# Second layer: the attention's values two slots ago, moved ahead of the scores on TensorE and their read ahead of the exponents on ScalarE

## The chip, the cores and the metric

The kernel runs on one core of one Trainium2 chip. The metric is the device time of the whole kernel in microseconds (us), as the median of several runs. Everything is computed in 32-bit floats apart from a few small helpers.

Engine names in the profile: PE is TensorE (matmuls; PEld are its weight loads), DVE is VectorE, ACT is ScalarE, POOL is GpSimd, SP is SyncE.

## The reference

Two transformer decoder layers over 16 sequences of 256 tokens of width 256 (4096 tokens). The change lies in the self-attention of the second layer:

```python
x = x + _L0_attn_ref(_layernorm(x, axis=-1), ...)
x = x + _L0_xattn_ref(_layernorm(x, axis=-1), ctx_1024, ...)
x = x + _L0_ffn_ref(_layernorm(x, axis=-1), ...)
x = x + _L1_attn_ref(_layernorm(x, axis=-1), L1_attn_Wq, L1_attn_Wkv_down, L1_attn_Wk_up, L1_attn_Wv_up, L1_attn_Wo)
x = x + _L1_xattn_ref(_layernorm(x, axis=-1), ctx_1024, ctx_1024, ...)
x = x + _L1_ffn_ref(_layernorm(x, axis=-1), L1_ffn_w_gate, L1_ffn_w_up, L1_ffn_w_down)

def _L1_attn_ref(x, Wq, Wkv_down, Wk_up, Wv_up, Wo):      # 8 heads of 64, latent width 64
    q = (x @ Wq.T).reshape(b, t, N_HEADS, HEAD_DIM)
    kv_latent = x @ Wkv_down.T
    k = (kv_latent @ Wk_up.T).reshape(b, t, N_HEADS, HEAD_DIM)
    v = (kv_latent @ Wv_up.T).reshape(b, t, N_HEADS, HEAD_DIM)
    scores = jnp.einsum('bqhd,bkhd->bhqk', q, k) * HEAD_DIM ** (-0.5)
    attn = jax.nn.softmax(scores, axis=-1)
    out = jnp.einsum('bhqk,bkhd->bqhd', attn, v)
    return out.reshape(b, t, N_HEADS * HEAD_DIM) @ Wo.T
```

## The kernel before

The program has four parts one after another: the first layer's attentions, its experts, `layer1` (the second layer's two attentions), and `feed_forward`. Only `layer1` is touched.

`layer1` works through eight groups g of 512 tokens (two sequences each). A group has eight slots s, one for each sequence b and pair of heads m; the slots are counted through all groups as t = 8g + s, and the last is t = 63 (`TAIL`). The keys' and values' up-projections are folded into the weights, so each slot multiplies absorbed queries with the 64-wide latent rows.

The order on each engine is written out by hand, as one loop over t for each engine, and each engine runs its row in order. Semaphores tie the rows together. What one slot's attention needs, in order:

- `scores(t)` (L1854, PE) fills banks P[0] and P[1]. It waits until the exponents of slot t-1 have read them.
- `maxima(t, e)` (L2206, DVE), one for each of the two heads e.
- `exponents(t)` (L2089, ACT), four of them, into `pr[t % 2]`, with their sums.
- `invert(t)` (L2211, DVE), and the product with the inverse sums (L1795, POOL), four of them.
- `turn(t)` (L1865, PE) transposes the rows into P[2] and P[3]. In the PE loop it stands in slot t+1.
- `by_key(t)`, the two copies of the turned rows into `PT[t % 2]`: ACT copies P[2] (L2102), DVE copies P[3] (L2217). Both stand in slot t+1 too, ACT's behind everything that ACT keeps in that slot.
- `values(t)` (L1880, PE) multiplies them with the latent rows into P[4]. It waits for both copies (`PTa_ready`, `PTd_ready`) and for the read of the slot before (`aT_ready`). In the PE loop it stands in slot t+2.
- `heads(t)` (L2096, ACT) reads P[4], also in slot t+2.

The other work of the layer is spread over the slots of a group as extras: in slot 0 the turn of the cross attention (L1966), the queries' fourth part (L1939) and the cross attention's values (L1977); in slot 1 the turn of the next group's normalised rows (L1890); in slot 2 the projection of the second sequence of the group before (L1948); in slot 3 the next group's latent (L1925); in slot 4 a turn of normalised rows, one of the latent keys (L1932) and queries; in slot 5 queries and a turn; in slot 6 queries and the cross attention's scores (L1958); in slot 7 a projection. They write the three banks P[5] to P[7] in turn; ACT empties most of them (`keep_unit`, L2077), and an extra waits until its bank is empty. ACT also normalises rows (L2115) at the end of slots 3 and 4.

Of the kernel before, what the change touches and what calls it, by code (L numbers as in the profile page):

```python
# [1581 lines left out]
def layer1(nc, ctx, c, io, dr):  # L1582

    st = ExitStack()
    with st:
# [67 lines left out]
        def group_step(t):  # L1653
            return t // NS, t % NS

        def there(i):
            return 0 <= i < NG
# [11 lines left out]
        TAIL = NS * Z + NS - 1  # L1669
# [59 lines left out]
        def wait_kept(e, name, i, parts=None):  # L1729
            k, _, n = place[name, i]  # L1730
            e.wait_ge(kept[k], n + (parts or after[name]))
# [3 lines left out]
        with nc.Block(no_gpsimd_drain=True) as block:  # L1735
# [79 lines left out]
            def _(p):  # L1815
# [25 lines left out]
                def scores(t):  # L1841
                    g, s = group_step(t)
                    b, m = s // NP, s % NP
                    if t == 0:
                        p.wait_ge(q.l_kept, 3 * (NG - NEARLY))
                        p.wait_ge(q.l_out_kept, NG - NEARLY)
                    if b == 0:
                        wait_kept(p, f"q{m}", g)
                    for u in range(2):
                        for e in range(2):  # L1850
                            if t and u == 0:
                                p.wait_ge(q.exp_ready, 4 * (t - 1) + 2 * e + 2)
                            r = slice(LR * e, LR * e + LR)
                            x = p.matmul(P[e][:, S * u:S * u + S], qT[g % 2][r, m, S * b + 128 * u:S * b + 128 * u + 128],  # L1854
                                         latT[g % 2][r, S * b:S * b + S], start=True, stop=True, tile_position=(LR * e, 0))
                    x.then_inc(q.s_psum, 1)
# [12 lines left out]
                def values(t):  # L1869
                    g, s = group_step(t)  # L1870
                    b = s // NP
                    if s == 0:
                        wait_kept(p, "latk", g)
                    p.wait_ge(q.PTa_ready, t + 1)
                    p.wait_ge(q.PTd_ready, t + 1)
                    if t:
                        p.wait_ge(q.aT_ready, t)
                    for k in range(2):
                        for e in range(2):
                            x = p.matmul(P[4][LR * e:LR * e + LR, 0:S], lat[g % 2][:, 2 * b + k, :], PT[t % 2][:, e, k, :],  # L1880
                                         start=(k == 0), stop=(k == 1), tile_position=(0, LR * e), skip_group_check=True)
                    x.then_inc(q.a_psum, 1)
# [59 lines left out]
                def project(i, b):  # L1942
                    name = f"project{b}"
                    p.wait_ge(q.aT_ready, NS * i + NP * b + NP)
                    room(p, name, i)
                    for j in range(2):
                        for m in range(NP):
                            x = p.matmul(bank(name, i)[:, D * j:D * j + D], aT[:, m, S * b + 128 * j:S * b + 128 * j + 128], wb[:, m, :],  # L1948
                                         start=(m == 0), stop=(m == NP - 1))
                    x.then_inc(full(name, i), 1)  # L1950
# [35 lines left out]
                for t in range(TAIL):  # L1986
                    g, s = group_step(t)
                    late, behind, ahead = there(g - 2), there(g - 1), there(g + 1)
                    scores(t)
                    if t == 0:  # L1990
                        queries(0, 1)
                        queries(0, 2)
                    if t >= 1:
                        turn(t - 1)
                    if t >= 2:
                        values(t - 2)
                    if s == 0 and late:
                        x_turn(g - 2)
                    if t == 1:
                        queries(0, 3)  # L2000
                    if s == 0 and behind:
                        queries(g, 3)
                    if s == 1 and ahead:
                        turn_norm(0, g + 1)
                    if s == 2 and behind:
                        project(g - 1, 1)
                    if s == 3 and ahead:
                        latent(g + 1)
                    if s == 4 and late:
                        turn_norm(2, g - 2)  # L2010
                    if s == 4 and ahead:
                        latent_keys(g + 1)
                    if s == 5 and ahead:
                        queries(g + 1, 1)
                    if s == 6 and ahead:
                        queries(g + 1, 2)
                    if s == 0 and late:
                        x_values(g - 2, 0)
                        x_values(g - 2, 1)
                    if s == 4 and ahead:  # L2020
                        queries(g + 1, 0)
                    if s == 5 and behind:
                        turn_norm(1, g - 1)
                    if s == 6 and behind:
                        x_scores(g - 1)
                    if s == 7:
                        project(g, 0)
                scores(TAIL)
                turn(TAIL - 1)
                values(TAIL - 2)  # L2030
                project(Z, 0)
                turn(TAIL)
                x_turn(Z - 1)
# [21 lines left out]
            def _(a):  # L2055
# [27 lines left out]
                def exponents(t):  # L2083
                    for e in range(2):
                        a.wait_ge(q.nmax_ready, 2 * t + e + 1)
                        if t >= 2:
                            a.wait_ge(q.pt_psum, 2 * (t - 2) + e + 1)
                        for u in range(2):
                            a.activation(pr[t % 2][:, e, u, :], P[e][:, S * u:S * u + S], ACT.Exp, bias=nmax[t % 2][:, e, u:u + 1],  # L2089
                                         accum_out=sums[t % 2][:, e, u:u + 1]).then_inc(q.exp_ready, 1)  # L2090

                def heads(t):
                    _, s = group_step(t)
                    b, m = s // NP, s % NP
                    a.wait_ge(q.a_psum, t + 1)
                    a.activation(aT[:, m, S * b:S * b + S], P[4][:, 0:S], ACT.Copy).then_inc(q.aT_ready, 1)  # L2096
# [28 lines left out]
                for t in range(TAIL):  # L2125
                    g, s = group_step(t)
                    late, behind, ahead = there(g - 2), there(g - 1), there(g + 1)
                    exponents(t)
                    if t in (0, 1):
                        keep_unit(f"q{t + 2}", 0, qT[0][:, t + 2, :], bank(f"q{t + 2}", 0)[:, :])  # L2130
                    if t >= 2:
                        heads(t - 2)
                    if s == 0 and late:
                        keep_unit("xturn", g - 2, xPT[:, :], bank("xturn", g - 2)[0:S2, :])
                    if s == 0 and behind:
                        keep_unit("q3", g, qT[g % 2][:, 3, :], bank("q3", g)[:, :])
                    if s == 1 and ahead:
                        keep_norm(0, g + 1, [hT0[:, u, :] for u in range(2)])
                    if s == 3 and ahead:
                        keep_unit("lat", g + 1, latT[(g + 1) % 2][:, :], bank("lat", g + 1)[:, :])  # L2140
                    if s == 4 and late:
                        keep_norm(2, g - 2, [c.hT_all[:, u, T * (g - 2):T * (g - 2) + T] for u in range(2)])
                    if s == 5 and ahead:
                        keep_unit("q0", g + 1, qT[(g + 1) % 2][:, 0, :], bank("q0", g + 1)[:, :])
                        keep_unit("q1", g + 1, qT[(g + 1) % 2][:, 1, :], bank("q1", g + 1)[:, :])
                    if s == 6 and behind:
                        keep_norm(1, g - 1, [hT[:, u, :] for u in range(2)])
                    if s == 6 and ahead:
                        keep_unit("q2", g + 1, qT[(g + 1) % 2][:, 2, :], bank("q2", g + 1)[:, :])
                    if t >= 1:  # L2150
                        by_key(t - 1)
                    if s == 3 and late:
                        normalise(2, g - 2, x5)
                    if s == 4 and behind:
                        normalise(1, g - 1, x4[(g - 1) % 2])
                    if s == 7 and behind:
                        x_exponents(g - 1)
# [839 lines left out]
```

## Time and profile before

| | |
|---|---|
| time, median of 3 runs | 1672.96 us (1669.79 to 1673.18) |
| profiled execution, own time | 1675.36 us |
| its span | 1673.6 us |
| `layer1`'s slots | from 932.9 us to about 1331 us of the span |
| PE busy, over the span | 1536.0 us (92%) |
| DVE, ACT, POOL busy | 979.0, 842.2, 468.4 us |
| mean granted clock of PE | 0.968 |

The page's slices show one fortieth of the span (41.8 us) in each digit; slices 23 to 32 hold the slots of `layer1`:

```profile
PE   8999999998987899999999899999999989996299
ACT  4446555555555422211212565666656533597980
PEclk9999999999998999999999999999999889998599
```

A digit 9 means busy for 90% or more; the line PEclk gives the granted clock in tenths of full speed. An average over a slice hides waits shorter than a few us, so the slots are read one by one below.

### The profile page before, as it was taken

What the parts mean: (1) busy time and instruction counts of PE and PEld (TensorE: products, weight loads), DVE (VectorE), ACT (ScalarE), POOL (GpSimd) and SP (SyncE); (2) the same over time, 40 slices, a digit from 0 to 9 for tenths busy, and PEclk for the clock granted to TensorE, in tenths of its full rate; (3) what the DMA queues carried; (4) which work ended last, traced back from release to release, by engine and by line L of the source; (5) the groups of instructions that cost most, each with busy time, mean ns of one, the idle gap of its engine ahead of it and who ended that gap; (6) DMA issues with size and microseconds to landing.
All of it is one profiled execution on the core that took longest, in us unless ns stands there. A gap on an engine that the chain in (4) does not pass through costs nothing. (4 is left out here: it accounts for less than half of the span.)

```text
span 1673.6 us, 27432 instructions
## 1 busy us (share of the span) xinstructions
PE 1536.0 (92%) x10279; PEld 1083.3 (65%) x10279; DVE 979.0 (58%) x2296; ACT 842.2 (50%) x1849; POOL 468.4 (28%) x592
## 2 busy tenths in 40 slices
PE   8999999998987899999999899999999989996299
PEld 5676767766755777787777466666666654442288
DVE  3665766767766435222222567766664568777883
ACT  4446555555555422211212565666656533597980
POOL 4223234253234410000002665555542300032100
PEclk9999999999998999999999999999999889998599
DMA  3440111011151154334424211110100000000031
GB/s 115 156 156 18 47 30 44 30 47 44 34 165 39 61 164 137 125 113 126 153 87 136 70 39 52 43 34 27 39 14 14 1 25 1 0 1 15 24 99 65
DMA packets 100929, 108.32 MB, mean 65 GB/s; under 512 B 25410, under 2 KB 89804, under 8 KB 100800
## 3 DMA queue, kind: packets, MB, share of 16 engines
q1 hardware_dynamic: 94656, 90.01, 17.3%
q0 software_dynamic: 6144, 16.57, 3.1%
q8 instruction: 83, 1.36, 0.3%
q14 instruction: 46, 0.38, 0.1%
HBM read 64.77 MB, written 42.01 MB: 64 GB/s over the span
## 5 line engine op out<-in xcount | busy, mean ns | idle before, releaser
L1795 POOL TENSOR_SCALAR c_pr<-c_pr,c_rsum 128x256 f32<-128x256 f32 x256 | 128.2, 518 | 190.2 <-DVE c_rsum L2211 189.8
L2089 ACT ACTIVATE c_pr<-bank,c_nmax 128x256 f32<-128x256 f32 x256 | 118.0, 473 | 119.9 <-DVE c_nmax L2206 119.8
L1526 ACT ACTIVATE b_G<-bank 128x320 f32<-128x320 f32 x128 | 56.0, 437 | 210.8 <-PE bank L1475 210.8
L1475 PE MATMUL bank<-b_XT,shared 128*128 128x320 f32 x512 | 154.6, 437 | 0.0
L2206 DVE TENSOR_REDUCE c_nmax<-bank 128x2 f32<-128x512 f32 x128 | 82.4, 685 | 108.6 <-PE bank L1854 108.5
L1489 PE MATMUL bank<-shared,b_G 128*128 128x256 f32 x640 | 142.2, 379 | 0.0
L1489 PEld LDWEIGHTS bank<-shared,b_G 128*128 128x128 f32 x640 | 120.9, 190 | 17.8
L1072 DVE TENSOR_TENSOR hT_all<-bank,a_causal 128x512 f32<-128x512 f32 x128 | 79.4, 682 | 67.5 <-PE bank L563 67.5
L498 POOL TENSOR_TENSOR a_L<-a_L,a_Lm 128x1232 f32<-128x1232 f32 x32 | 72.0, 2249 | 149.5 <-DVE a_Lm L1087 149.5
L1475 PEld LDWEIGHTS bank<-b_XT,shared 128*128 128x128 f32 x512 | 92.5, 193 | 27.6 <-issue 1.2
L1545 DVE COPY b_Y<-bank 128x256 f32<-128x256 f32 x80 | 33.9, 424 | 120.3 <-PE bank L1489 120.1
L1537 DVE COPY b_XT<-bank 128x256 f32<-128x256 f32 x80 | 34.0, 424 | 100.0 <-PE bank L1462 100.0
L1754 POOL MEMSET c_minus<- 128x4 f32 x1 | 0.1, 102 | 309.1 <-POOLq L54 309.1
L1865 PE MATMUL bank<-ident,c_pr 128*128 128x128 f32 x512 | 73.2, 283 | 12.5 <-POOL c_pr L1795 10.0
L2650 PE MATMUL bank<-wdT,d_raw 128*128 128x256 f32 x384 | 83.1, 379 | 0.9 <-DVE d_raw L2897 0.9
L2593 PE MATMUL bank<-hT_all,wuT 128*128 128x512 f32 x192 | 82.9, 593 | 0.0
L2593 PE MATMUL bank<-hT_all,wgT 128*128 128x512 f32 x192 | 82.6, 592 | 0.0
L2650 PEld LDWEIGHTS bank<-wdT,d_raw 128*128 128x128 f32 x384 | 72.9, 190 | 11.0 <-DVE d_raw L2897 1.1
L1865 PEld LDWEIGHTS bank<-ident,c_pr 128*128 128x128 f32 x512 | 55.5, 142 | 37.7 <-POOL c_pr L1795 25.6
L690 PE MATMUL bank<-ident,a_L 128*77 128x128 f32 x512 | 66.9, 282 | 12.4 <-ACT a_L L943 7.2
L1854 PE MATMUL bank<-c_latT,c_qT 64*128 64x256 f32 x512 | 75.5, 407 | 0.6 <-ACT c_qT L2077 0.4
L513 POOL DMA_INDIRECT t_slots_in<-a_h,a_slot_s x64 | 63.3, 989 | 30.0 <-issue 17.1
(376 smaller groups left out, 3400.2 us busy)
## 6 DMA issues: line engine op xcount, KB each, us to landing
shared<-L_ffn_w SPq DMA_DIRECT2D x32, 512.0 KB, 6.0
t_slots_in<-a_h SPq DMA_DIRECT2D x20, 512.0 KB, 7.5
shared<-t_slots_in SPq DMA_DIRECT2D x15, 640.0 KB, 7.3
t_slots_out<-b_Y SPq DMA_DIRECT2D x15, 640.0 KB, 4.1
hT_all<-x SPq DMA_DIRECT2D x8, 512.0 KB, 4.0
a_xr<-x SPq DMA_DIRECT2D x8, 512.0 KB, 3.9
t_x_a<-a_x SPq DMA_DIRECT2D x8, 512.0 KB, 2.9
shared<-t_x_a SPq DMA_DIRECT2D x8, 512.0 KB, 4.3
```

The source lines that it names most:

```text
L498: p.tensor_tensor(L[n % 2][:, :, :], L[n % 2][:, :, :], bcast(Lm[n % 2][:, :], 2, S2), ALU.subtract).then_inc(q.sub_ready, 1)
L690: x = p.transpose(bank(name, i)[0:S2, 128 * k:128 * k + 128], L[n % 2][:, 4 * rg + k, :], ident)
L1072: v.tensor_tensor(A[:, rg, :, :, :].rearrange("p e k t -> p (e k) t"), P[rg][:, :].rearrange("p (n t) -> p n t", t=128), bcast(causal[:, : ...
L1475: t = p.matmul(P[2 + n % 2][:, 0:HC], w1[e % 3][:, u, 128 * f:128 * f + 128], XT[e % 2][:, u, HC * m:HC * m + HC], start=(u == 0), stop=(u ...
L1489: t = p.matmul(P[4 + n % 3][:, 0:D], G[e % 2][:, f, 128 * j:128 * j + 128], w2[e % 3][:, f, :], start=(f == 0), stop=(f == 3))
L1795: p.tensor_scalar(pr[k][:, e, u, :], pr[k][:, e, u, :], rsum[k][:, e, u:u + 1], 1.0, ALU.mult, ALU.mult).then_inc(q.pr_ready, 1)
L1854: x = p.matmul(P[e][:, S * u:S * u + S], qT[g % 2][r, m, S * b + 128 * u:S * b + 128 * u + 128], latT[g % 2][r, S * b:S * b + S], start=Tr ...
L1865: x = p.transpose(P[2 + e][:, S * k + 128 * u:S * k + 128 * u + 128], pr[t % 2][:, e, u, 128 * k:128 * k + 128], ident)
L2089: a.activation(pr[t % 2][:, e, u, :], P[e][:, S * u:S * u + S], ACT.Exp, bias=nmax[t % 2][:, e, u:u + 1], accum_out=sums[t % 2][:, e, u:u ...
L2206: v.tensor_reduce(nmax[t % 2][:, e, :], P[e][:, :].rearrange("p (u k) -> p u k", u=2), AX.X, ALU.max, negate=True).then_inc(q.nmax_ready, 1)
L2593: t = p.matmul(bank[:, :], wT[:, u, 128 * f:128 * f + 128], hT[:, u, T * g:T * g + T], start=(u == 0), stop=(u == 1))
L2650: t = p.matmul(P[n % 8][:, 0:D], raw[:, f, T * g + 128 * j:T * g + 128 * j + 128], wdT[:, f, :], start=(f == 0), stop=(f == FC - 1))
```

## The change

On PE, `values(t - 2)` moves from behind `turn(t - 1)` to ahead of `scores(t)`, in every slot from the third on, and in the tail. On ACT, `heads(t - 2)` moves from behind the exponents (and, in the first slots, a keep) to ahead of them; ACT's tail stays. DVE, POOL and SP keep their rows. No instruction is added or taken out, and all waits stay with their instructions.

```diff
@@ PE
                 for t in range(TAIL):
                     g, s = group_step(t)
                     late, behind, ahead = there(g - 2), there(g - 1), there(g + 1)
+                    if t >= 2:
+                        values(t - 2)
                     scores(t)
                     if t == 0:
                         queries(0, 1)
                         queries(0, 2)
                     if t >= 1:
                         turn(t - 1)
-                    if t >= 2:
-                        values(t - 2)
                     if s == 0 and late:
                         x_turn(g - 2)
...
+                values(TAIL - 2)
                 scores(TAIL)
                 turn(TAIL - 1)
-                values(TAIL - 2)
                 project(Z, 0)
@@ ACT
                 for t in range(TAIL):
...
+                    if t >= 2:
+                        heads(t - 2)
                     exponents(t)
                     if t in (0, 1):
                         keep_unit(f"q{t + 2}", 0, qT[0][:, t + 2, :], bank(f"q{t + 2}", 0)[:, :])
-                    if t >= 2:
-                        heads(t - 2)
```

PE's row in a steady group, from the turn in slot 1 to the turn in slot 3 (L1865 turn, L1880 values, L1890 turn of normalised rows, L1854 scores, L1948 projection). Before:

```order
L1865 MATMUL bank<-ident,c_pr 128x128 x8
L1880 MATMUL bank<-c_PT,c_lat 64x256 x4
L1890 MATMUL bank<-ident,c_h 128x128 x8
L1854 MATMUL bank<-c_latT,c_qT 128x256 x4
L1865 MATMUL bank<-ident,c_pr 128x128 x8
L1880 MATMUL bank<-c_PT,c_lat 64x256 x4
L1948 MATMUL bank<-c_wb,shared 128x256 x8
L1854 MATMUL bank<-c_latT,c_qT 128x256 x4
L1865 MATMUL bank<-ident,c_pr 128x128 x8
```

And after the change, over the same stretch:

```order
L1865 MATMUL bank<-ident,c_pr 128x128 x8
L1890 MATMUL bank<-ident,c_h 128x128 x8
L1880 MATMUL bank<-c_PT,c_lat 64x256 x4
L1854 MATMUL bank<-c_latT,c_qT 128x256 x4
L1865 MATMUL bank<-ident,c_pr 128x128 x8
L1948 MATMUL bank<-c_wb,shared 128x256 x8
L1880 MATMUL bank<-c_PT,c_lat 64x256 x4
L1854 MATMUL bank<-c_latT,c_qT 128x256 x4
L1865 MATMUL bank<-ident,c_pr 128x128 x8
```

The values that stood behind the turn of their slot now close the slot before it: between the turn of a slot's rows and its values stand the extras of one slot alone, where before there were also a set of scores and another turn.

ACT's row over slots 3 and 4 of a steady group (L2089 exponents, L2096 read of the heads, L2077 keeps, L2102 copy, L2115 normalised rows). Before:

```order
L2089 ACTIVATE c_pr,c_sums<-bank,c_nmax 128x256 x4
L2096 ACTIVATE shared<-bank 128x256
L2077 ACTIVATE c_latT<-bank 128x512
L2102 ACTIVATE c_PT<-bank 128x512
L2115 ACTIVATE c_h<-c_x,c_shift,c_rstd 128x256 x4
L2089 ACTIVATE c_pr,c_sums<-bank,c_nmax 128x256 x4
L2096 ACTIVATE shared<-bank 128x256
L2077 ACTIVATE hT_all<-bank 128x512 x2
L2102 ACTIVATE c_PT<-bank 128x512
```

And after:

```order
L2096 ACTIVATE shared<-bank 128x256
L2089 ACTIVATE c_pr,c_sums<-bank,c_nmax 128x256 x4
L2077 ACTIVATE c_latT<-bank 128x512
L2102 ACTIVATE c_PT<-bank 128x512
L2115 ACTIVATE c_h<-c_x,c_shift,c_rstd 128x256 x4
L2096 ACTIVATE shared<-bank 128x256
L2089 ACTIVATE c_pr,c_sums<-bank,c_nmax 128x256 x4
L2077 ACTIVATE hT_all<-bank 128x512 x2
L2102 ACTIVATE c_PT<-bank 128x512
```

The read of the heads stands ahead of the exponents; the copy L2102 keeps its place at the end of the slot's keeps.

## Rows read from the trace of the kernel before

**Rows 1.** Windows, one steady group: length, busy us (count) of each engine, PEclk, DMA share, GB/s

```profile
1127.18:1178.96 51.78, 49.50 (x301) 32.27 (x302) 35.67 (x90) 33.08 (x108) 27.96 (x43) 1.00 0.11 32
```

**Rows 2.** Timeline, DVE, maxima of slots 0 to 7: start, us, engine, line, [idle before]

```profile
1127.18 1.29 DVE L2206 TENSOR_REDUCE c_nmax<-bank 128x2 f32<-128x512 f32 x2 [1.39 <-PE bank L1854]
...
1134.32 1.29 DVE L2206 TENSOR_REDUCE c_nmax<-bank 128x2 f32<-128x512 f32 x2 [2.49 <-PE bank L1854]
...
1138.45 1.29 DVE L2206 TENSOR_REDUCE c_nmax<-bank 128x2 f32<-128x512 f32 x2 [0.38 <-PE bank L1854]
...
1146.51 1.29 DVE L2206 TENSOR_REDUCE c_nmax<-bank 128x2 f32<-128x512 f32 x2 [2.47 <-PE bank L1854]
...
1151.53 1.29 DVE L2206 TENSOR_REDUCE c_nmax<-bank 128x2 f32<-128x512 f32 x2 [0.17 <-PE bank L1854]
...
1159.22 1.29 DVE L2206 TENSOR_REDUCE c_nmax<-bank 128x2 f32<-128x512 f32 x2 [2.21 <-PE bank L1854]
...
1165.11 1.29 DVE L2206 TENSOR_REDUCE c_nmax<-bank 128x2 f32<-128x512 f32 x2 [0.76 <-PE bank L1854]
...
1172.20 1.29 DVE L2206 TENSOR_REDUCE c_nmax<-bank 128x2 f32<-128x512 f32 x2 [2.31 <-PE bank L1854]
```

**Rows 3.** Timeline, PE, slot 1 and the start of slot 2

```profile
1135.23 1.08 PE L1880 MATMUL bank<-c_PT,c_lat 128*64 128x256 f32 x8
...
1136.24 1.09 PE L1890 MATMUL bank<-ident,c_h 128*128 128x128 f32 x8
...
1137.26 1.14 PE L1854 MATMUL bank<-c_latT,c_qT 64*128 64x256 f32 x8
...
1139.17 0.66 PE L1865 MATMUL bank<-ident,c_pr 128*128 128x128 f32 x4 [0.77 <-POOL c_pr L1795]
```

**Rows 4.** Timeline, ACT and DVE, slot 1

```profile
1135.04 0.47 ACT L2089 ACTIVATE c_pr<-bank,c_nmax 128x256 f32<-128x256 f32 x1 [2.44 <-DVE c_nmax L2206]
...
1136.86 0.40 ACT L2096 ACTIVATE shared<-bank 128x256 f32<-128x256 f32 x1
1137.12 1.11 ACT L2077 ACTIVATE c_hT<-bank 128x512 f32<-128x512 f32 x2
...
1137.30 0.68 DVE L2217 COPY c_PT<-bank 128x512 f32<-128x512 f32 x1
...
1138.08 0.64 ACT L2102 ACTIVATE c_PT<-bank 128x512 f32<-128x512 f32 x1
```

**Rows 5.** Timeline, PE and ACT, slots 3 and 4

```profile
1148.43 1.98 PE L1925 MATMUL bank<-c_hT,shared 128*128 128x512 f32 x4
...
1150.45 0.60 ACT L2077 ACTIVATE c_latT<-bank 128x512 f32<-128x512 f32 x1 [1.00 <-PE bank L1925]
...
1150.95 0.59 ACT L2102 ACTIVATE c_PT<-bank 128x512 f32<-128x512 f32 x1
...
1153.39 0.46 ACT L2089 ACTIVATE c_pr<-bank,c_nmax 128x256 f32<-128x256 f32 x1
...
1156.12 1.98 PE L1939 MATMUL bank<-c_hT,c_wa 128*128 128x512 f32 x4 [0.95 <-ACT hT_all L2077]
```

**Rows 6.** Timeline, PE weight loads, slot 6 of the group before

```profile
1117.30 1.86 PEld L1958 LDWEIGHTS bank<-hT_all,c_hT 128*128 128x128 f32 x16 [0.90 <-ACT c_hT L2077]
```

**Rows 7.** All maxima (first, last start); first maximum of group 2, of group 7

```profile
L2206 DVE TENSOR_REDUCE c_nmax<-bank x128: 673/681/693, 932.9 to 1326.9; 128x2 f32<-128x512 f32 x128
...
1023.62 0.69 DVE L2206 TENSOR_REDUCE c_nmax<-bank 128x2 f32<-128x512 f32 x1 [1.39 <-PE bank L1854]
...
1282.50 0.69 DVE L2206 TENSOR_REDUCE c_nmax<-bank 128x2 f32<-128x512 f32 x1 [3.38 <-PE bank L1854]
```

**Rows 8.** Windows and timeline of PE in group 7: two stretches, and a hole

```profile
1295.60:1299.00 3.40, 3.40 (x14) 1.84 (x13) 2.54 (x11) 1.29 (x6) 1.74 (x4) 0.50 0.00 0
...
1321.69 2.57 PE L1958 MATMUL bank<-hT_all,c_hT 128*128 128x77 f32 x16 [1.51 <-ACT c_hT L2077]
...
1322.90:1329.60 6.70, 6.70 (x31) 4.67 (x30) 2.54 (x6) 1.94 (x8) 0.32 (x1) 0.50 0.01 2
```

## The prediction

> **What bounds the kernel now.** I read the page's slices first: TensorE (PE) sits at nine tenths nearly everywhere. The change touches only the self-attention of the second layer, from 932.95 us on, so I then read one group of it. A group of 512 tokens is eight slots, and groups 2 to 6 repeat to 0.02 us. In one of them PE is busy for 49.50 of 51.78 us at clock 1.00, ACT for 33.08 and DVE for 35.67 [rows 1]: PE sets the rate, and at most about 2.3 us a group can be won. The start of DVE's first maximum marks each slot, since it follows the end of PE's scores. Its starts, and the end of the group's window, give these slot lengths for slots 0 to 7: 7.14, 4.13, 8.06, 5.02, 7.69, 5.89, 7.09, 6.76, in sum 51.78 [rows 1, 2]. I call that start M and give all times within a slot from its M.
>
> Two slots hold stalls of PE. In slot 2 the turn waits 0.77 us, then again, for POOL's normalised rows, because slot 1 was short [rows 3]; slot 7 holds the same pieces without a wait (turn, values, one projection, scores) and takes 6.76, so slot 2 loses 8.06 - 6.76 = 1.3 us. In slot 4 the queries wait 0.95 us for ACT to clear a bank [rows 5], because ACT's four normalisations (L2115) push its exponents to 1153.39 - 1151.53 = 1.86 instead of the usual 0.72 (1135.04 - 1134.32) [rows 2, 4, 5].
>
> **The change part by part.** No instruction is added or removed. Before, PE's row was scores(t), turn(t-1), values(t-2), then the slot's other pieces ("extras"). Now values(t-2) stand ahead of scores(t), so they come right behind the extras of slot t-1. What values(t-2) need are the two copies of the turned rows, ACT's L2102 and DVE's L2217, and both are made in slot t-1. Before, the extras, scores(t) and turn(t-1) lay between turn(t-2) and these values; now only the extras do. And the scores queue behind them, although the banks that they write are free once the exponents have read them at about 2.6. That is the added wait: behind it stand scores(t), then the maxima, the exponents, POOL's products and the next turn, that is the whole chain.
>
> I work out each slot twice: a PE path (all its pieces without a stall) and a copy path. The copy path is the end of ACT's copy, then about 0.07 to PE (an estimate; the last maximum reaches ACT as fast), 1.01 of values (1136.24 - 1135.23) and 1.19 from the start of the scores to M (1138.45 - 1137.26 [rows 2, 3]), together 2.27. ACT's read of the heads, which took 0.26 between exponents and keeps (1137.12 - 1136.86 [rows 4]), now lies ahead of the exponents in ACT's idle time, so the copies come 0.26 earlier. Extras and the keeps that wait for them come 1.01 earlier, since no values stand before them.
>
> Slot 0: ACT's copy waits for the keep of the queries, for which PE is ready 1.01 earlier; PE's four extras after it hide the copy. Stays 7.14.
> Slot 1: copy ended at 1138.08 + 0.64 - 1134.32 = 4.40, now 4.14; DVE's ended at 3.66 [rows 4] and is covered. Copy path 6.41 against a PE path of 4.13: +2.28.
> Slot 2: slot 1 is now long enough for POOL, the stall goes. PE path 6.76: -1.30. What is late next is ACT's copy at 3.15 (exponents until 1136.86 - 1134.32 = 2.54, then 0.6), path 5.4, hidden by the projection.
> Slot 3: the copy ended at 1150.95 + 0.59 - 1146.51 = 5.03 behind the latent's keep, which waited 1.00 us for PE [rows 5]; both come 1.01 earlier, so 4.02, path 6.29: +1.27.
> Slot 4: with slot 3 longer and L2115 begun earlier the exponents start at 0.72. ACT clears the awaited bank at 2.54 + 0.65 = 3.2; then the queries 1.91 (1159.22 - 1156.12 - 1.19), values 1.01, scores 1.19: 7.31, -0.38.
> Slot 5: exponents to 2.54, two keeps and the copy as in slot 1 (1138.08 + 0.64 - 1137.12 = 1.60, and the keeps wait for nothing now): 4.14 to 4.26, path 6.5: +0.6.
> Slot 6: the context scores wait for ACT's keeps even now (start 3.97: 1117.30 with 0.90 of waiting [rows 6], less that group's M, 1165.11 - 51.78 = 1113.33). Values no longer fill that wait. Start 3.70, 1.93 of work (7.09 - 3.97 - 1.19), then 2.20: 7.83, +0.74.
> Slot 7: the projection, 6.76 - 4.13 + 1.02 = 3.7 us long (slot 1 has a turn of the norm in its place, 1.02 by 1137.26 - 1136.24), hides the copies: 6.76.
> Sum 7.14 + 6.41 + 6.76 + 6.29 + 7.31 + 6.5 + 7.83 + 6.76 = 55.0, or +3.2 a group, 16 for groups 2 to 6.
>
> Groups 0 and 1 took 1023.6 - 932.9 = 90.7 [rows 7]. They have fewer extras (nothing of the cross attention of a group two back), so PE is free sooner, but the copies are no sooner: no slot can be shorter than 3.15 + 2.27 = 5.4. With the same paths group 1 comes to 52 and group 0 to 49 (its second slot an estimate, at 8): +10. Group 7 has seven such slots from 1282.5 to the last slot's M, one maximum (0.6) before 1326.9: 43.8 [rows 7]; by the paths 44.8, +1. So the waits alone cost 16 + 10 + 1 = 27 us, between 21 (copies 0.1 us sooner in all of the slots) and 32 (0.2 us of pipeline refill where values follow long matmuls, 25 times).
>
> **The clock.** Slot 1 gets a hole in PE from the end of the norm's turn (about 1.9) to the values (4.2), 2.3 us long; slots 3 and 6 get about 1.3 and 1.0. The trace has a fall of the clock to 0.50 (1.2 of 2.4 GHz) just behind a hole of 1.51 us, lasting 6.7 us, and another of 3.4 us [rows 8]; the holes of 0.77 and 0.95 in the steady groups left it at 1.00 [rows 1, 3, 5]. 3.4 us at half clock take 1.7 us of work, 6.7 us take 3.35, at most. Slot 2 behind the hole is bound by PE, so it is paid there nearly in full. A fall in each of eight groups would cost 8 x 1.7 = 14 to 27 us; none, 0. The hole lies well above 1.51, but one case is thin ground for saying that each such hole brings a fall, so I take about six falls, less the two that group 7 already has in this stretch: 4 x 1.7 = 7 us. On this the Trainium skill, "TensorE: Matmul & The Clock Gate", section "A second HAM failure mode: psum-queue depth-cycling", says that small idle times between groups of matmuls, made by cycling through banks, are enough to make the clock swing back and forth. By it the steady groups should swing already; the trace, with 1.00 over a whole group, does not agree for holes under 1 us and agrees for 1.51.
>
> Sum: 27 + 7 = 34 over the profiled execution's 1675.36 us (span 1673.6 and 1.8 around it), 1709. The median of the runs is 2.4 lower, so 1707.
>
> **The rivals.** (a) The waits come as worked out and the clock holds: +27, 1700. For it: five steady groups of before never fell. Against: the hole is three times theirs. (b) The clock falls in nearly every group, some for 6.7 us: +27 + 8 x 2.5 = +47, less 3 for those of before: 1717. This is the side to which the skill's rule points. (c) Faster: if the copies were in time (ACT's copy ended before the extras do), only the stalls of slots 2 and 4 would change. They go, PE runs at its busy time, and 7 groups win 1.3 + 0.95 each, 16 us: 1657. It decides at the point where ACT's copy ends before 1.9 in slot 1 and 2.6 in slot 3; the rows have 4.40 and 5.03, later than the exponents alone allow (2.54), so it is nearly excluded. (d) The order changes nothing, because lengthened short slots are just repaid by shortened long ones: 1673. For it: slots 2 and 4 repay 1.9 us a group. Against: slots 1, 3, 5 and 6 add 4.9.
>
> **How the numbers follow.** Forecast (waits, about six falls; 1701 to 1711) 0.50; (a) with 1692 to 1701 0.25; (b) with 1711 to 1722 0.19; (d) 0.03; (c) 0.03. The range from 1692 to 1721 leaves out (c), (d) and the tails. A difference under 0.2% (3.3 us) can't be told from none here: faster 0.03, same 0.03, slower 0.94.
>
> **What would show it.** Right: slots 1, 3, 5 and 6 of a steady group at about 6.4, 6.3, 6.5 and 7.8; PE idle ahead of L1880 with ACT's L2102 as releaser, near 2.3 us in slot 1, where before L1880 waited for nothing; no wait for POOL in slot 2 any more; exponents of slot 4 at 0.72; stretches at clock 0.50 behind slot 1 in some groups. Wrong: if L1880 starts right behind the extras, (c) holds; if a steady group is 54 to 55 us and the clock is 1.00 throughout, (a); if the group lasts over 58, (b) or a cost that I have not seen, such as a slower start of values behind 512-column matmuls.

## The result, and the profile after

The changed kernel takes 1701.89 us (median of 5 runs, 1701.09 to 1706.67) against 1673.18 us (5 runs of the kernel before): 28.7 us slower by the medians (1.72%). The recorded ratio is 1.0184, 95% interval 1.0165 to 1.0203. The forecast was 1707, range 1692 to 1721. The profiled execution took 1701.09 us, its span is 1699.4 us.

First the window of one steady group, from the first maximum of its slot 0 to that of the next group's (length, busy us and count of PE, PEld, DVE, ACT, POOL, then the granted clock). It answers to [rows 1].

```profile
1140.25:1194.68 54.43, 48.66 (x301) 32.17 (x302) 35.07 (x89) 33.64 (x108) 28.00 (x44) 1.00 0.10 30
```

PE does the same instructions in 0.8 us less of busy time, but the group lasts 54.43 instead of 51.78 us. Where it goes is read from the timeline of DVE's maxima, which answers to [rows 2]:

```profile
1140.25 1.29 DVE L2206 TENSOR_REDUCE c_nmax<-bank 128x2 f32<-128x512 f32 x2 [1.20 <-PE bank L1854]
...
1147.55 1.29 DVE L2206 TENSOR_REDUCE c_nmax<-bank 128x2 f32<-128x512 f32 x2 [2.65 <-PE bank L1854]
...
1153.98 1.29 DVE L2206 TENSOR_REDUCE c_nmax<-bank 128x2 f32<-128x512 f32 x2 [2.67 <-PE bank L1854]
...
1160.53 1.29 DVE L2206 TENSOR_REDUCE c_nmax<-bank 128x2 f32<-128x512 f32 x2 [1.71 <-PE bank L1854]
...
1166.60 1.29 DVE L2206 TENSOR_REDUCE c_nmax<-bank 128x2 f32<-128x512 f32 x2 [1.22 <-PE bank L1854]
...
1173.91 1.29 DVE L2206 TENSOR_REDUCE c_nmax<-bank 128x2 f32<-128x512 f32 x2 [2.80 <-PE bank L1854]
...
1180.28 1.29 DVE L2206 TENSOR_REDUCE c_nmax<-bank 128x2 f32<-128x512 f32 x2 [1.25 <-PE bank L1854]
...
1188.12 1.29 DVE L2206 TENSOR_REDUCE c_nmax<-bank 128x2 f32<-128x512 f32 x2 [3.05 <-PE bank L1854]
```

The differences of the starts (the last against the window's end) give the slots:

| slot | 0 | 1 | 2 | 3 | 4 | 5 | 6 | 7 | group |
|---|---|---|---|---|---|---|---|---|---|
| before | 7.14 | 4.13 | 8.06 | 5.02 | 7.69 | 5.89 | 7.09 | 6.76 | 51.78 |
| predicted | 7.14 | 6.41 | 6.76 | 6.29 | 7.31 | 6.5 | 7.83 | 6.76 | 55.0 |
| measured | 7.30 | 6.43 | 6.55 | 6.07 | 7.31 | 6.37 | 7.84 | 6.56 | 54.43 |

What makes slots 1, 3 and 5 long is seen in the list of waits over the whole stage, from 926 to 1356 us (engine, line, what it waited for, us in total, times, longest):

```profile
ACT shared L2096 <- PE bank L1880: 80.1, 53, 3.0
PEld bank L1880 <- ACT c_PT L2102: 34.3, 22, 2.6
PE bank L1880 <- ACT c_PT L2102: 31.9, 27, 2.4
...
PE bank L1865 <- POOL c_pr L1795: 0.8, 2, 0.5
```

The values (L1880), which in the kernel before never waited for ACT's copy (L2102) in this stage, now wait 31.9 us for it. POOL's products hold up the turn for 0.8 us, all of it in slot 1 of group 0; before, it was 10.0 us. The wait of the heads' read (L2096) is long and free: it lies ahead of the exponents, where ACT has nothing else to do (in a steady group they still start 0.72 to 0.73 us behind the maxima). Slots 1 and 3 on the timeline, to be held beside [rows 3 to 5]:

```profile
1147.44 1.09 PE L1865 MATMUL bank<-ident,c_pr 128*128 128x128 f32 x8
...
1148.37 0.60 PE L1890 MATMUL bank<-ident,c_h 128*128 128x128 f32 x4
...
1149.89 0.66 PE L1890 MATMUL bank<-ident,c_h 128*128 128x128 f32 x4 [0.93 <-DVE c_x L2339]
...
1151.08 0.60 ACT L2102 ACTIVATE c_PT<-bank 128x512 f32<-128x512 f32 x1
...
1151.78 1.08 PE L1880 MATMUL bank<-c_PT,c_lat 128*64 128x256 f32 x8 [1.23 <-ACT c_PT L2102]
...
1163.76 0.59 ACT L2102 ACTIVATE c_PT<-bank 128x512 f32<-128x512 f32 x1
...
1164.40 1.08 PE L1880 MATMUL bank<-c_PT,c_lat 128*64 128x256 f32 x8 [1.17 <-ACT c_PT L2102]
```

In both slots the copy ends (1151.68 and 1164.35), and 0.1 or 0.05 us later the values start. In slot 1 the hole is in two pieces: the second half of the norm's turn first waits 0.93 us for DVE to read a bank.

Over the whole stage the starts of the maxima, first and last, answer to the first line of [rows 7]:

```profile
L2206 DVE TENSOR_REDUCE c_nmax<-bank x128: 678/686/693, 928.3 to 1354.8; 128x2 f32<-128x512 f32 x128
```

426.5 us against 394.0, that is 32.5 more; the stage began 4.6 us earlier in this execution. The code ahead of it is the same in all kernels here, and in the profiled executions shown below it ended between 927.0 and 934.3. In this spread small effects on the total drown, so the stage is compared by itself where it matters.

### The profile page after: what moved, and what is told of

It reads as the page before. It is cut to its first block and busy times, and to the rows that moved or that the text cites. A ratio compares the mean times of both kernels' runs of the same rounds, so it can differ in the third digit from the quotient of the medians.

```text
span 1699.4 us, 27432 instructions
## 1 busy us (share of the span) xinstructions
PE 1532.4 (90%) x10279; PEld 1088.6 (64%) x10279; DVE 976.5 (57%) x2296; ACT 846.6 (50%) x1849; POOL 468.6 (28%) x592
## 5 line engine op out<-in xcount | busy, mean ns | idle before, releaser
L2089 ACT ACTIVATE c_pr<-bank,c_nmax 128x256 f32<-128x256 f32 x256 | 118.0, 473 | 93.0 <-DVE c_nmax L2206 93.0
L1880 PE MATMUL bank<-c_PT,c_lat 128*64 128x256 f32 x512 | 73.8, 411 | 35.4 <-ACT c_PT L2102 31.9
L1880 PEld LDWEIGHTS bank<-c_PT,c_lat 128*64 128x64 f32 x512 | 33.2, 142 | 70.7 <-ACT c_PT L2102 34.4
L1854 PE MATMUL bank<-c_latT,c_qT 64*128 64x256 f32 x512 | 76.3, 419 | 0.4 <-ACT c_qT L2077 0.4
L690 PEld LDWEIGHTS bank<-ident,a_L 128*77 128x77 f32 x512 | 59.2, 154 | 21.4 <-ACT a_L L943 8.9
```

Of the source, the lines that this page charges most:

```text
L690: x = p.transpose(bank(name, i)[0:S2, 128 * k:128 * k + 128], L[n % 2][:, 4 * rg + k, :], ident)
```

## The experiments

"Stage" is the time from the first to the last maximum: 394.0 before, 426.5 changed. All experiments keep the arithmetic; only orders change, and the two filled kernels add transposes that nobody reads.

**Values between scores and turn, ACT as before.** Run twice, on two chips.

```diff
                     scores(t)
+                    if t >= 2:
+                        values(t - 2)
                     if t >= 1:
                         turn(t - 1)
-                    if t >= 2:
-                        values(t - 2)
@@ tail
                 scores(TAIL)
+                values(TAIL - 2)
                 turn(TAIL - 1)
-                values(TAIL - 2)
```

> The kernel before, with the values moved only past the turn: scores(t), values(t-2), turn(t-1). ACT keeps its order. Theory (the loss of the change is that the scores queue behind values that wait for ACT's copy): here nothing stands between the exponents' end and the scores, the copies are as old as before, so no wait on L1880; the turn comes 1.0 us later, which covers 1.0 of the 1.3 us that slot 2 waited for POOL. Slot 2 of a steady group 7.1 instead of 8.06, group 50.8, total 7 us under before, 1666. Rival (values do best right behind the turn, as a later turn makes both copies and the inverse sums late): at least one slot grows by 0.5 or more and the total is 1673 or above.

> The version with values between scores and turn once more, as the partner of the next run on one chip: stage of the slots 369.7 us as before, total 1653 to 1657.

Measured: 1654.61 us against 1670.66, ratio 0.9904 (0.9887 to 0.9922), and again 1656.73 against 1669.69, ratio 0.9931 (0.9912 to 0.9949). It beats both kernels, and by more than the theory had (1666). Stage 378.4 and 377.5:

```profile
L2206 DVE TENSOR_REDUCE c_nmax<-bank x128: 673/681/693, 927.0 to 1305.4; 128x2 f32<-128x512 f32 x128
```

A steady group takes 50.01 us: 6.99, 4.11, 7.05, 4.83, 7.68, 5.69, 7.10, 6.56. Slot 2 is shorter by the 1.0 us expected, though its values do wait 0.43 us for ACT's copy, where no wait was expected. The rest, 0.76 us a group, comes in slots 0, 3, 5 and 7, in which nothing of PE waited before. Groups 0, 1 and 7 bring the other 6.7 us; in group 7 the fall of the clock behind the holes of slot 2 is gone. PE in slot 7, first before, then here:

```profile
1172.09 1.09 PE L1865 MATMUL bank<-ident,c_pr 128*128 128x128 f32 x8
...
1173.11 1.08 PE L1880 MATMUL bank<-c_PT,c_lat 128*64 128x256 f32 x8
...
1174.12 3.72 PE L1948 MATMUL bank<-c_wb,shared 128*128 128x256 f32 x16
...
1177.78 1.13 PE L1854 MATMUL bank<-c_latT,c_qT 64*128 64x256 f32 x8
```

```profile
1157.90 1.08 PE L1880 MATMUL bank<-c_PT,c_lat 128*64 128x256 f32 x8
...
1158.92 1.09 PE L1865 MATMUL bank<-ident,c_pr 128*128 128x128 f32 x8
...
1159.74 1.38 PEld L1948 LDWEIGHTS bank<-c_wb,shared 128*128 128x128 f32 x7
...
1159.85 3.62 PE L1948 MATMUL bank<-c_wb,shared 128*128 128x256 f32 x16
...
1163.39 1.13 PE L1854 MATMUL bank<-c_latT,c_qT 64*128 64x256 f32 x8
```

The turn has the tile 128*128, the values 128*64, the projection 128*128. Behind the turn the projection's weights begin to load 0.82 us after the turn's start, while the turn still runs (its row lasts 1.09). Behind a step of another tile shape nothing starts before 1.01 or 1.02 us. From the turn's start to the scores are 1177.78 - 1172.09 - 1.01 = 4.68 us without the values before, and 4.47 here. In this order, and in that of the change, one switch of tile shape fewer is made in a slot: 0.2 us each. The Trainium skill, "TensorEngine Tiling (Array Packing)", section "Key Properties", says that a change of tiling mode drains the engine. The trace agrees: the next weights wait for the running matmuls only where the shape changes, and the price is 0.2 us. The tile 128*77 of slot 0 counts as the turn's own shape: its weights too begin to load 0.82 us after the turn's start (1116.29 - 1115.47).

**One switch put back, in slot 7 of that kernel.**

```diff
-                    if t >= 2:
+                    if t >= 2 and s != 7:
                         values(t - 2)
...
-                def project(i, b):
+                def project(i, b, between=None):
...
                     for j in range(2):
+                        if j and between is not None:
+                            values(between)
                         for m in range(NP):
...
                     if s == 7:
-                        project(g, 0)
+                        project(g, 0, t - 2)
```

> The version with values between scores and turn, but in slot 7 the values stand in the middle of the projection, between its two halves, so that PE changes the shape of its tiles four times in that slot (64*128 scores, 128*128 turn and half the projection, 128*64 values, 128*128 rest) plus the way back to the scores, as in the kernel before, and not once less. Theory (each change between tile shapes costs PE about 0.2 us more than a following instruction of the same shape): slot 7 is 6.75, as before the change, instead of 6.56; no other slot moves. Rival (the 0.2 us came from the turn not being followed by the values, or from other waits): slot 7 stays at 6.56.

Measured: slot 7 takes 6.75 us in groups 1 to 6 instead of 6.56, and no other steady slot moves by over 0.02. There is one run alone, 1656.28 us, so the total says nothing; the slots do. PE there:

```profile
1162.00 1.09 PE L1865 MATMUL bank<-ident,c_pr 128*128 128x128 f32 x8
1162.93 1.89 PE L1950 MATMUL bank<-c_wb,shared 128*128 128x256 f32 x8
1164.75 1.08 PE L1880 MATMUL bank<-c_PT,c_lat 128*64 128x256 f32 x8
```

The projection follows the turn, of the same shape, after 0.93 us, and its first half is followed by the values. The price of a switch, 0.19 us, is shown.

**PE's half of the change alone.** The read of the heads is put back behind the exponents.

```diff
-                    if t >= 2:
-                        heads(t - 2)
                     exponents(t)
                     if t in (0, 1):
                         keep_unit(...)
+                    if t >= 2:
+                        heads(t - 2)
```

> The changed kernel with ACT's read of the heads put back behind the exponents; PE as changed. Theory (ACT's copy ends last, and the read ahead of the exponents brings it forward by 0.26 us): slots 0, 1, 4, 5, 6 each about 0.26 longer than changed, steady group 55.6, total 1708 to 1711. Rival (the read of the heads ahead of the exponents is what costs in the change): faster than the changed kernel, near 1673 to 1690.

Measured: 1721.01 us, ratio 1.0308 (1.0283 to 1.0333). The waits are as expected: a group without a fall of the clock is 55.89 us, slots 0, 1, 4, 5 and 6 are 0.27 to 0.28 longer than changed. The total is 10 us above the expected range. Three of the five steady groups have a fall of the clock, at 1.6 us each, where the changed kernel has none; that is 4.9 us. Its stage is 439.4 us, 13.0 above the changed kernel's, of which the five steady slots make 7.3. Another 4.5 us of the profiled execution lie ahead of the stage, in identical code. Slot 1 of group 4 (timeline and window of the fall):

```profile
1160.08 1.98 PE L1880 MATMUL bank<-c_PT,c_lat 128*64 128x256 f32 x8 [1.50 <-ACT c_PT L2102]
1161.98 1.88 PE L1854 MATMUL bank<-c_latT,c_qT 64*128 64x256 f32 x8
...
1160.00:1163.40 3.40, 3.32 (x14) 2.11 (x16) 0.00 (x0) 0.00 (x0) 2.93 (x5) 0.52 0.38 127
```

The hole ahead of the values is 1.50 us, not 1.23, and the values and scores behind it take nearly double, so this slot lasts 8.33 instead of 6.69. The same hole of 1.50 stands in slot 1 of all five steady groups, and a fall followed in two of them only; the third fall came behind a hole of 1.32 in slot 6. The rival falls: ACT's half is what helps.

**ACT's half alone.**

> The kernel before, with only ACT's move: the read of the heads ahead of the exponents, PE as before. Theory: the read now waits for values(t-2), which end about 2.0 us behind the start of the maxima, so the exponents start at about 2.3 instead of 0.72 and the short slots grow; steady group about 55, total 1695 to 1705. So each half alone is bad and the ACT half helps only with the PE half. Rival (ACT's move is harmless in itself): within 3 us of 1673.

Its diff is the ACT part of the change. Measured: 1726.98 us, ratio 1.0322 (1.0296 to 1.0348), above the expected 1695 to 1705. The mechanism is as expected; slot 1 of a steady group:

```profile
1162.98 1.29 DVE L2206 TENSOR_REDUCE c_nmax<-bank 128x2 f32<-128x512 f32 x2 [1.64 <-PE bank L1854]
...
1165.02 0.39 ACT L2096 ACTIVATE shared<-bank 128x256 f32<-128x256 f32 x1 [4.23 <-PE bank L1880]
1165.30 0.47 ACT L2089 ACTIVATE c_pr<-bank,c_nmax 128x256 f32<-128x256 f32 x1
```

The exponents start 2.32 us after the maxima. The size was wrong: a steady group takes 57.9 to 58.3 us, not 55. Slots 0, 1, 3, 5 and 6 grow by 0.73 to 1.46, slot 2 shrinks by 0.63; that makes 56.7, and each steady group has a fall of the clock besides.

**ACT's copy first in slots 1, 3 and 5**, on the changed kernel.

```diff
+                FIRST_COPY = (1, 3, 5)
                 for t in range(TAIL):
...
+                    if t >= 1 and s in FIRST_COPY:
+                        by_key(t - 1)
                     if s == 0 and late:
...
-                    if t >= 1:
+                    if t >= 1 and s not in FIRST_COPY:
                         by_key(t - 1)
```

> The changed kernel, with ACT's copy of the turned rows (L2102) ahead of its keeps in slots 1, 3 and 5. Theory (in these slots the values wait for that copy alone): the copy ends at 3.15 behind M instead of 4.1, 3.8 and 4.1; slot 1 goes from 6.42 to 5.9 to 6.4 (DVE's copy at 3.66, or the turn of the norm, becomes the last), slot 3 from 6.07 to 5.4, slot 5 from 6.37 to 5.9 to 6.4; group 53.0 to 53.8 instead of 54.4, total 6 to 14 us under the changed kernel, 1688 to 1696. Rival (the start of the values is set by PE itself or by the read of the heads): slots 1, 3, 5 and the total as in the changed kernel, 1702.

Measured: 1696.62 us, ratio 1.0167 (1.0151 to 1.0184), 5.3 us under the changed kernel and just short of the 6 to 14 expected; the two intervals overlap, so the totals alone do not show a gain. The stage is 415.3, 11.2 under the changed kernel: 4.5 from the steady slots, the rest from groups 0, 1 and 7 and from three falls of the clock instead of four ahead of slot 62. Slot 3 goes from 6.07 to 5.39, slot 1 from 6.43 to 6.11, slot 5 from 6.37 to 6.46 (no gain; the second half of its turn of rows now waits 0.55 us for the later keep). A group is 53.52 us. In slot 1 the last wait is no longer for ACT's copy but for DVE's, which is L2220 in this kernel:

```profile
1149.18 1.08 PE L1880 MATMUL bank<-c_PT,c_lat 128*64 128x256 f32 x8 [0.92 <-DVE c_PT L2220]
...
1161.13 1.08 PE L1880 MATMUL bank<-c_PT,c_lat 128*64 128x256 f32 x8 [0.50 <-ACT c_PT L2102]
```

So ACT's copy was the last wait in slots 1 and 3, as the prediction had it; with it moved ahead, the values of slot 3 start 0.67 us sooner behind the slot's first maximum.

**Holes filled with transposes**, on the changed kernel: first eight at the end of slot 1 and six in slot 6, then more, at fewer places (this second form is shown).

```diff
+        FILL = {2: 14, 10: 14, 58: 18, 60: 14, 61: 6, 62: 6}
...
+                    if t in FILL:
+                        if t > 2:
+                            p.wait_ge(q.aT_ready, t - 2)
+                        keep_busy(p, P[4], ident, FILL[t])
                     if t >= 2:
                         values(t - 2)
...
                     if s == 6 and behind:
+                        p.wait_ge(q.aT_ready, t - 1)
+                        keep_busy(p, P[4], ident, 7)
                         x_scores(g - 1)
```

> The changed kernel with transposes of the identity (128x128, read by nobody) in the two longest holes of PE: eight into the values' bank ahead of the values at the end of each slot 1, six ahead of the context scores in slot 6. Theory (the changed kernel pays 5 falls of the clock between 928 and 1350 us, 1.5 to 3 us each, against 2 before): the falls at the end of group 1 and in group 7 go, no slot gets longer, total 5 to 9 us under the changed kernel, 1693 to 1697. Rival (the falls have another reason, or transposes do not count as work for the clock): the clock falls in the same places and the total stays at 1702.

> The changed kernel with more transposes of the identity in its holes, and only where a fall of the clock was seen or near: ahead of the values, 14 at the end of slot 1 in groups 0 and 1, 18, 14, 6 and 6 at the ends of slots 1, 3, 4 and 5 of group 7, and 7 ahead of the context scores in each slot 6. Theory (the changed kernel's stage from the first maximum to the last slot is 415.6 us, of which 6 to 7 us are falls of the clock behind holes of over 2 us): no fall between the first and the last slot, slots 0 to 5 of group 7 at 7.3, 5.9, 6.6, 5.4, 6.4, 5.4, stage 409 us, total about 6 us under the changed kernel, 1695. Rival (transposes do not keep the clock up; the shorter filling brought only 2.3 us in the stage): falls behind the same slots, stage 412 to 416.

Measured: 1700.46 us, ratio 1.0170 (1.0149 to 1.0192), and 1700.95 us, ratio 1.0187 (1.0162 to 1.0213); neither differs from the changed kernel's 1.0184, where 1693 to 1697 and 1695 were expected. From the first maximum to the start of slot 62 (as the expectation counts) the changed kernel took 415.6 us, these 413.3 and 410.5. The second has slots 0 to 5 of group 7 at 7.30, 6.12, 6.56, 5.39, 6.37 and 5.39, as expected, and one fall that the changed kernel did not have, behind an unfilled hole of group 4 (1.5 us; without it 409.0, the theory's figure). The four falls that the changed kernel had in this stretch are gone. That transposes count as work for the clock is shown at the start of the program, where 44 of the same kind run with nothing else on PE. In the changed kernel, over 0 to 7.3 us and from 7.7 us (number, then shortest, median and longest in ns):

```profile
L175 PE MATMUL bank<-ident x24: 361/421/445, 2.3 to 7.2; 128*128 128x128 f32 x24
...
L175 PE MATMUL bank<-ident x19: 272/273/273, 7.5 to 9.5; 128*128 128x128 f32 x19
```

They run slow up to 7.36 us, where the granted clock rises, and fast behind it. That the filling is what kept the four falls away is likely but not shown: the unfilled hole of 2.94 us in slot 1 of group 7 was followed by a fall in the changed kernel and by none in the run with PE's half alone. The totals do not gain. The stages are 4.7 and 4.3 us shorter than the changed kernel's, but in these profiled executions they began 4.5 and 3.7 us later; why the medians do not move either is not shown. What the clock costs the changed kernel in its median is left open.

**ACT's copy first in slot 3, on the kernel with values between.** The diff is as above, with `(3,)`.

> Values between scores and turn, and ACT's copy (L2102) ahead of the latent's keep in slot 3 alone. Theory (in slot 4 PE waits 1.15 us for ACT, which is late because its normalisations at the end of slot 3 start behind the copy, and the copy behind the latent's keep): the copy no longer waits for PE's latent, the normalisations start 0.5 us earlier, the exponents of slot 4 at about 1.3 instead of 1.86, slot 4 7.2 instead of 7.69; 3 to 4 us in all, 1651 against 1654.6 for the version without it. Rival (slot 4 is bound by the normalised rows' other inputs from POOL and DVE): no slot moves, 1654 to 1655.

> The same with ACT's copy ahead of the latent's keep in slot 3, on the same chip as the run before. The stage of the slots was 366.9 against 369.7 us in the traces, but the medians, from two chips, 1656.5 against 1654.6. Theory (the 2.8 us are real and drown in the spread of the stages ahead, which differed by 7 us between executions of identical code): total 1 to 4 us under its partner. Rival (something behind the slots pays it back): total equal or above, with a longer stretch from the last slot to the end.

Measured: 1656.51 us (ratio 0.9920, 0.9904 to 0.9935) and, beside its partner, 1654.26 us (0.9917, 0.9896 to 0.9938) against 1656.73. The first lies above the 1651 expected, the second 2.5 us under its partner, as expected. In the trace slot 4 takes 7.20 instead of 7.69, its exponents start at 1.38 instead of 1.86, and up to the start of slot 62 both executions are shorter: 366.9 and 366.6 us against 369.7 and 369.8. Over the whole stage less is left, 376.2 and 376.1 against 378.4 and 377.5, because slot 62 lasts 8.73 and 8.97 us with a fall of the clock of 6.8 us in it, against 8.16 and 7.10 without the change. So 2.8 to 3.3 us are won in the slots and part is paid back in the last one. The intervals of the totals overlap, so as a gain of the kernel it is likely and not shown.

## Why the prediction was right

The direction and the mechanism were right, and the time lies in the range, 5 us under the forecast. Part of how near it came is luck: two errors of the sum, one up and one down, partly cancel. By its steps:

- **The added wait and the slots.** Shown: all eight slots within 0.22 us, L1880 waiting for L2102, and the run with the copy first. In slot 6 the context scores wait 1.04 us for ACT's keeps, as worked out. The sum of the slots was 55.0, measured 54.43, so 13 us for groups 2 to 6 where 16 were expected.
- **What made the sum too large** is a term that it lacked: one switch of tile shape fewer per slot, 0.2 us. It fits slots 2 and 7 (6.55 and 6.56 for 6.76), which are bound by PE, and slot 3, where the latent and all behind it come 0.2 earlier. Its upper bound had named a refill where values follow long matmuls; slots 2 and 7, where values follow the projection, show none beyond the switch that the scores paid before.
- **Slot 0** was put at no change and grew by 0.16. The context values come so early that the load of their weights now waits 0.88 us for ACT's `xPT`; they start 1.93 us behind the queries, before it was 1.72.
- **The stalls of slots 2 and 4.** The wait for POOL is gone from the steady groups. Slot 4 is 7.31 as worked out, with its exponents at 0.72; its queries still wait 0.96 us for ACT, only sooner in the slot.
- **Groups 0 and 1** took 103.1 us against 90.7. Two falls of the clock are in it, 1.5 and 1.6 us, so the waits cost 9.3 where 10 were charged.
- **The two falls of before were taken off twice.** Group 7 was charged +1 against 43.8 us, which is its measured length with both falls in it; the term of the clock then took them off once more. With that put right the same steps give 3.4 us more, 1710.
- **The clock.** Falls came in slots 1 and 6 of group 1 and slots 1, 3 and 6 of group 7: five, where about six were expected. They cost 8.8 us of the stage: 3.1 in group 1, and 5.7 in group 7, whose seven slots took 50.6 us and would take 45.0 by the fall-free slots of the filled runs (44.8 by the paths). The waits then make 13.2 + 9.3 + 1.2 = 23.7 us where 27 were charged. The place of the falls was wrong. They were expected behind slot 1 of the steady groups, where none fell. The hole of 2.3 us is in two pieces of 0.93 and 1.23 there; that this is the reason is not shown, since in one of the filled runs the same two pieces were followed by a fall. In group 1 it is in one piece:

```profile
983.91 1.04 PE L1890 MATMUL bank<-ident,c_h 128*128 128x128 f32 x8
987.33 1.97 PE L1880 MATMUL bank<-c_PT,c_lat 128*64 128x256 f32 x8 [2.38 <-ACT c_PT L2102]
...
987.00:990.40 3.40, 3.08 (x14) 1.85 (x16) 0.00 (x0) 0.61 (x2) 2.93 (x5) 0.50 0.13 36
```

- **How long a hole has to be.** The prediction went by 1.51 us and held that holes under 1 us leave the clock alone. The trace of before has the counterexample: its fall at 1295.6 came behind two waits for POOL in slot 2 of group 7. In the changed kernel the fall in slot 6 of group 1 came behind a hole of 1.04 us, which stands in slot 6 of each steady group without one:

```profile
1294.48 0.66 PE L1865 MATMUL bank<-ident,c_pr 128*128 128x128 f32 x4 [0.99 <-POOL c_pr L1795]
1295.39 0.96 PE L1865 MATMUL bank<-ident,c_pr 128*128 128x128 f32 x4 [0.25 <-POOL c_pr L1795]
```

```profile
1019.10 1.98 PE L1958 MATMUL bank<-hT_all,c_hT 128*128 128x77 f32 x16 [1.04 <-ACT c_hT L2077]
```

- **The rivals.** By the prediction's own sign, a steady group of 54 to 55 us at clock 1.00, the five steady groups are as in (a); groups 1 and 7 fall as in the forecast. The measured 1701.9 lies on the border between the two.
- **The total.** The profiled stage grew by 32.5 us, where 34 were forecast, and the whole by 25.7, since the identical part ahead of it ran 4.6 us shorter in that execution and the rest 2.2 less. The medians say 28.7. What stands between 32.5 and 28.7 in them is not shown.

## What to carry to other kernels

In an order written by hand, ask of each step how long ago its inputs were made and who queues behind it. Values that were three steps old were moved to where they were one step old, in front of the scores, and so every wait for them became a wait of the whole chain. A step whose inputs are old belongs directly behind the step that starts the critical chain, here between scores and turn: that gave 0.7 to 1.0%, and let POOL finish meanwhile. Two halves of a change can each be bad alone: ACT's half by itself made the slowest kernel here (1726.98 us), and beside PE's it was worth 19 us (7.3 of them in the waits of the steady groups).

## What the runs showed of the hardware

- A change of PE's tile shape between steps (64*128, 128*64, 128*128) costs 0.19 to 0.2 us: the next weights do not load under the running matmuls.
- The length of a hole in PE does not by itself decide on a fall of the clock. In the changed kernel holes of 0.93 to 1.23 us left it at 1.00 in all five steady groups, but in group 1 a hole of 1.04 was followed by a fall, and in a filled run the pair of 0.93 and 1.22. Holes of 1.50 in slot 1 of the kernel with PE's half alone were followed by a fall in two of five steady groups. Of the changed kernel's six holes of 2.2 us and more, four were. The hole of 2.0 us in slot 62 of the kernel with values between brought a fall in one execution and none in the other.
- One fall of 3.4 us costs 1.5 to 1.6 us.
- Transposes of the identity raise the clock like other work: with nothing else on PE they went from 421 to 273 ns each at 7.36 us.
- The same code ahead of the stage ended within a range of 7 us between executions.
